# Tile 30's image-prompt softmax: which of its steps run on GpSimd and which on VectorE

## The chip, the core and the metric

The kernel runs on one core of a Trainium2 chip. The core has a matrix engine (TensorE, PE in the profile; PEld is its weight loads), three elementwise engines (VectorE = DVE, ScalarE = ACT, GpSimd = POOL) and SyncE (SP), which here only issues DMAs. Each engine runs its own instruction list in order; engines wait for each other through counting semaphores. An instruction whose semaphore has not arrived holds up everything behind it on its engine. The metric is the device time of one execution in microseconds, the median of several.

## The reference

Eight batches of 512 tokens with 320 channels attend, with 20 heads of 16 channels, to 60 text tokens and 4 image-prompt ("ip") tokens of 512 channels. Cut to what matters:

```python
q = heads(x @ W_q)
probs_t  = softmax(q @ k_t.T * scale)                 # 60 text tokens
text_out = probs_t @ v_t
qsem  = l2norm(probs_t @ text_ehs)                    # direction of the attended text
sem   = qsem @ l2norm(ip_ehs).T                       # 4 numbers a head
fused = q @ k_ip.T * scale + 0.5 * sem
probs_ip = softmax(fused) * spatial_mask              # over the 4 ip tokens
out = (text_out + probs_ip @ v_ip) @ W_out + b_out + x
```

The kernel takes the ip logits relative to the fourth ip token, so three numbers a head (60 columns for 20 heads) are computed and the fourth is a zero that was written once. The norm of `qsem` comes from a quadratic form of the unnormalised text probabilities with a 60x60 Gram matrix, one number a head.

## The kernel before, in words

The 4,096 tokens are 32 tiles of 128 (tiles 0 to 31). A tile is worked in five units of four heads, 160 units in all (units 0 to 159; tile 30 has units 150 to 154, tile 31 units 155 to 159). For each unit TensorE forms scores (`scores`), VectorE takes their maximum (`maxima`), ScalarE their exponentials (`exps`), TensorE transposes those (`e_transposes`), ScalarE copies them (`copy_eT`), TensorE multiplies them by a table of Gram matrix, ip directions and values (`table_products`), VectorE forms four quadratic forms (`quadratic`, line 795, one custom instruction and one accumulator read each), and ScalarE copies the rest of the product (`copy_fin`, line 628).

When a tile's five units are through, its end steps follow. Their names and lines:

- `clamp` on VectorE (lines 939, 942, 943): a guarded quadratic form, and the reciprocal of the text softmax's sum. From the first, ScalarE's `norms` (725, 727) makes the inverse norm, a logarithm and an exponential.
- `normalize` on GpSimd (516): the text part of the output row, written into `mixed` (320 columns).
- semn, sum, maximum, centring: ip directions times the inverse norm, plus the ip logits, their maximum over four, and the difference from it. On VectorE these are the four instructions of `centre` (949, 952, 954, 956); on GpSimd they are `fuse` (524, 527) and `centre` (533), with the maximum alone on VectorE (923).
- `weights` on ScalarE (732): the exponential.
- `weigh`: sum, reciprocal, weighting with the mask, written into `mixed` beside the text part. On VectorE three instructions (963, 965, 967); on GpSimd the last is two (541, 545), while sum and reciprocal stay on VectorE.
- Then TensorE transposes the row (`attn_transposes`, 1086), ScalarE copies it rounded (`attn_high`, 633), VectorE takes what rounding lost (`attnT_lows`, 877), TensorE multiplies by the output weights (`out_project`, 1108, nine matmuls), VectorE adds the residual (`add_residual`, 884) and SP stores the tile.

Tiles 0 to 27 go through the end steps in pairs, tiles 28 to 31 singly. Their groups are numbered in `POST`; `PLAIN` is 16, tile 30's group, and `PLAIN + 1` tile 31's. Before the change the GpSimd form of the end steps is used up to tile 29 (whose weighting is already on VectorE), and the VectorE form for tiles 30 and 31.

No scheduler sets the order. Each engine's list is written out in Python, as `slot(u)` calls with extra steps hung in at given values of `u`. Three orders matter at the end. On VectorE: `quadratic(156)`, `clamp` of tile 30, `quadratic(157)`, `centre` of tile 30, the residual of tile 28, `quadratic(158)`, `attnT_lows(29)`, `weigh` of tile 30, `quadratic(159)`, then the end steps of tile 31 with `attnT_lows(30)` ahead of their `centre`. On TensorE: `table_products(159)`, `attn_transposes(30)`, `out_project(29)`, `out_project(30)`, then the transposes and products of tile 31 (1115, 1123, 1125, 1128, 1130). `attn_transposes(30)` waits for `attn_made` and for `pip_made`, the semaphore that tile 30's weighting raises, and `out_project(29)` stands behind it. On GpSimd only the two `normalize` of tiles 30 and 31 remain.

Of the kernel before, what the change touches and what calls it, by code (L numbers as in the profile page):

```python
# [31 lines left out]
ALU = mybir.AluOpType  # L32
ACT = mybir.ActivationFunctionType
AX_X = mybir.AxisListType.X
# [10 lines left out]
def xattn_kernel(nc, x, ctx_tokens, ip_mask, w_q, w_k, w_v, w_k_ip, w_v_ip, w_out, b_out, out):  # L45
# [18 lines left out]
    ALL_UNITS, ALL_TILES, ALL_HALVES = B * UNITS, B * TILES, B * HALVES  # L64
# [11 lines left out]
    PLAIN = len(POST) - 2  # L76
# [4 lines left out]
    with es:  # L81
# [6 lines left out]
        def sem(name):  # L88
            return es.enter_context(nc.semaphore(name))
# [9 lines left out]
        def again(place, *shape):  # L99

            start = place_used.get(place.name, 0)
            place_used[place.name] = start + math.prod(shape)
            names = "abc"[:len(shape)]
            return place[:, start:start + math.prod(shape)].rearrange(
                f"p ({' '.join(names)}) -> p {' '.join(names)}", **dict(zip(names, shape)))
# [61 lines left out]
        fused = again(place_wq, TILES, HEADS, NIP)  # L167
        ipmax = again(place_ctxT, TILES, HEADS)
        ipd = again(place_wq, TILES, HEADS, NIP)
        ipe = again(place_ctxT, TILES, HEADS, NIP)  # L170
        ipsum = again(place_ctxT, TILES, HEADS)
        iprec = again(place_ctxT, TILES, HEADS)
# [53 lines left out]
        rnorm_made, semn_made, fused_made = sem("rnorm_made"), sem("semn_made"), sem("fused_made")  # L226
        attn_made, ipmax_made, ipd_made, ipe_made = (
            sem("attn_made"), sem("ipmax_made"), sem("ipd_made"), sem("ipe_made"))
        ipsum_made, iprec_made, ipw_made, pip_made = (
            sem("ipsum_made"), sem("iprec_made"), sem("ipw_made"), sem("pip_made"))  # L230
# [3 lines left out]
        end_step = sem("end_step")  # L234
# [33 lines left out]
        def ring(g):  # L268

            t, n = POST[g]  # L270
            return slice(t % TILES, t % TILES + n)
# [110 lines left out]
        def _(pool):  # L382
            g = nc.gpsimd
# [128 lines left out]
            def normalize(g):  # L512

                n, tiles = POST[g][1], ring(g)
                pool.wait_ge(rsum_made, g + 1)
                nc.gpsimd.tensor_tensor(  # L516
                    mixed[:, tiles, 0:C].rearrange("p t (h d) -> p t h d", d=D), fin[:, tiles, :, NDIF:NDIF + D],
                    rsum[:, tiles].unsqueeze(3).to_broadcast([P, n, HEADS, D]), ALU.mult).then_inc(attn_made, 1)
# [10 lines left out]
            def centre(g):  # L529

                n, tiles = POST[g][1], ring(g)
                pool.wait_ge(ipmax_made, g + 1)
                nc.gpsimd.tensor_tensor(ipd[:, tiles], fused[:, tiles], ipmax[:, tiles].unsqueeze(3).to_broadcast([P, n, HEADS, NIP]),
                                        ALU.subtract).then_inc(ipd_made, 1)

            def weigh(g):

                (t, n), tiles = POST[g], ring(g)
                pool.wait_ge(iprec_made, g + 1)
                pool.sem_inc(pool_turn, 1)  # L540
                nc.gpsimd.tensor_tensor(ipw[:, tiles], iprec[:, tiles],
                                        mask_sb[:, t % TILES:t % TILES + n].unsqueeze(2).to_broadcast([P, n, HEADS]),
                                        ALU.mult).then_inc(ipw_made, 1)
                pool.wait_ge(ipw_made, g + 1)
                nc.gpsimd.tensor_tensor(
                    mixed[:, tiles, C:C + IPCOLS].rearrange("p t (h n) -> p t h n", n=NDIF), ipe[:, tiles, :, 0:NDIF],
                    ipw[:, tiles].unsqueeze(3).to_broadcast([P, n, HEADS, NDIF]), ALU.mult).then_inc(pip_made, 1)
# [21 lines left out]
            for g in range(SINGLE // 2, PLAIN):  # L569
# [3 lines left out]
                fuse(g)  # L573
                centre(g)
            normalize(PLAIN)
            normalize(PLAIN + 1)


        @block.scalar
        def _(act):  # L580
# [49 lines left out]
            def attn_high(t):  # L630

                act.wait_ge(attnT_done, t + 1)
                nc.scalar.copy(attn_parts(t)[0], mi_ps[:, misc_bank(("at", 0, t)), 0:QC * P]).then_inc(attnT_hi, 1)
# [88 lines left out]
            def norms(g):  # L722

                act.wait_ge(quadc_made, g + 1)
                nc.scalar.activation(lnq[:, ring(g)], quadc[:, ring(g)], ACT.Ln).then_inc(lnq_made, 1)
                act.wait_ge(lnq_made, g + 1)
                nc.scalar.activation(rnorm[:, ring(g)], lnq[:, ring(g)], ACT.Exp, scale=-0.5).then_inc(rnorm_made, 1)

            def weights(g):

                act.wait_ge(ipd_made, g + 1)
                nc.scalar.activation(ipe[:, ring(g)], ipd[:, ring(g)], ACT.Exp).then_inc(ipe_made, 1)

            for u in range(ALL_UNITS + 2):
                slot(u)
                if u == ALL_UNITS - 2:
                    norms(PLAIN)
                if u == ALL_UNITS - 1:
                    weights(PLAIN)
            attn_high(ALL_TILES - 2)  # L740
            norms(PLAIN + 1)
            weights(PLAIN + 1)

            act.wait_ge(last_done, 1)
# [6 lines left out]
        def _(dve):  # L751
            v = nc.vector
# [120 lines left out]
            def attnT_lows(t):  # L873

                dve.wait_ge(attnT_hi, t + 1)
                high, low = attn_parts(t)
                v.tensor_tensor(low, mi_ps[:, misc_bank(("at", 0, t)), 0:QC * P], high.bitcast(F32), ALU.subtract).then_inc(attnT_lo, 1)
# [56 lines left out]
            def clamp(g):  # L934

                t = POST[g][0]
                dve.wait_ge(fin_copied, GROUPS * (t + 1))
                ssum = fin[:, ring(g), :, FINW - 1]
                v.scalar_tensor_tensor(out=guard[:, ring(g)], in0=ssum, scalar=EPS * EPS, in1=ssum,
                                       op0=ALU.mult, op1=ALU.mult).then_inc(guard_made, 1)  # L940
                dve.wait_ge(guard_made, g + 1)
                v.tensor_tensor(quadc[:, ring(g)], quad[:, ring(g)], guard[:, ring(g)], ALU.max).then_inc(quadc_made, 1)
                v.reciprocal(rsum[:, ring(g)], ssum).then_inc(rsum_made, 1)  # L943

            def centre(g):

                tiles, steps = ring(g), 3 * (g - PLAIN)
                dve.wait_ge(rnorm_made, g + 1)
                v.tensor_tensor(semn[:, tiles], fin[:, tiles, :, 0:NDIF],
                                rnorm[:, tiles].unsqueeze(3).to_broadcast([P, 1, HEADS, NDIF]), ALU.mult).then_inc(end_step, 1)  # L950
                dve.wait_ge(end_step, steps + 1)
                v.tensor_tensor(fused[:, tiles, :, 0:NDIF], semn[:, tiles], sip[:, tiles], ALU.add).then_inc(end_step, 1)
                dve.wait_ge(end_step, steps + 2)
                v.tensor_reduce(ipmax[:, tiles], fused[:, tiles], AX_X, ALU.max).then_inc(end_step, 1)
                dve.wait_ge(end_step, steps + 3)
                v.tensor_tensor(ipd[:, tiles], fused[:, tiles], ipmax[:, tiles].unsqueeze(3).to_broadcast([P, 1, HEADS, NIP]),
                                ALU.subtract).then_inc(ipd_made, 1)

            def weigh(g):

                t = POST[g][0]
                dve.wait_ge(ipe_made, g + 1)
                v.tensor_reduce(ipsum[:, ring(g)], ipe[:, ring(g)], AX_X, ALU.add).then_inc(ipsum_made, 1)
                dve.wait_ge(ipsum_made, g + 1)
                v.reciprocal(iprec[:, ring(g)], ipsum[:, ring(g)]).then_inc(iprec_made, 1)
                dve.wait_ge(iprec_made, g + 1)
                v.scalar_tensor_tensor(
                    out=mixed[:, t % ARING, C:C + IPCOLS].rearrange("p (h n) -> p h n", n=NDIF), in0=ipe[:, t % TILES, :, 0:NDIF],
                    scalar=mask_sb[:, t % TILES:t % TILES + 1], in1=iprec[:, t % TILES].unsqueeze(2).to_broadcast([P, HEADS, NDIF]),
                    op0=ALU.mult, op1=ALU.mult).then_inc(pip_made, 1)  # L970

            for u in range(ALL_UNITS + 1):
                slot(u)
                if u == ALL_UNITS - 4:
                    weigh(PLAIN - 1)
                if u == ALL_UNITS - 3:
                    clamp(PLAIN)
                if u == ALL_UNITS - 2:
                    centre(PLAIN)
                if u == ALL_UNITS - 1:  # L980
                    weigh(PLAIN)

            clamp(PLAIN + 1)
            attnT_lows(ALL_TILES - 2)
            centre(PLAIN + 1)
            weigh(PLAIN + 1)
            dve.wait_ge(last_hi, 1)
            v.tensor_tensor(last_attnT_low[:, 0:2 * P], LAST_ATTN[:, 0:2 * P], last_attnT[:, 0:2 * P].bitcast(F32),
# [302 lines left out]
```

## Time and profile before

| what | value |
|---|---|
| median of 3 runs | 318.04 us (317.91, 318.04, 320.0) |
| the profiled execution | 319.01 us, of which its span is 317.3 us |
| PE, DVE, ACT busy, share of the span | 95%, 85%, 87% |
| POOL busy | 66% |
| the change begins to act | about 305 us into the span |

The span runs from the first to the last instruction of the profiled execution; the 1.71 us beside it lie around it. Busy shares are averages over the whole span. The change touches only the last 13 us, where the shares are others: there the rows of single instructions, in order of time, say who waits for whom. Times in such rows are us from the span's start.

### The profile page before, as it was taken

How to read it: one execution, taken by the hardware profiler on the slowest of the kernel's cores; microseconds unless marked ns; L12 is line 12 of the kernel's file. 1: busy time of each engine (PE TensorE's matmuls, PEld its weight loads, DVE VectorE, ACT ScalarE, POOL GpSimd, SP SyncE). 2: the span in 40 equal slices, each digit the busy share in tenths (PEclk: the TensorE clock that was granted, in tenths of full speed). 3: DMA queues.
4: the chain of work that ended last, by engine and by line, in shares of the span. 5: the costliest groups of instructions: out<-in, count | busy, mean ns of one | idle time of the engine just before them, and what ended most of it. 6: DMA issues, size and time to landing. Idle time of an engine off the chain costs nothing.

```text
span 317.3 us, 8813 instructions
## 1 busy us (share of the span) xinstructions
PE 301.7 (95%) x2289; PEld 291.1 (92%) x2289; DVE 269.5 (85%) x1861; ACT 276.9 (87%) x1168; POOL 210.1 (66%) x372
## 2 busy tenths in 40 slices
PE   4899899999999999999999999999999999998976
PEld 3789769888999999999999999999999999998964
DVE  5483846798889898989898989998999899898995
ACT  3744679999999999999999999999999999999942
POOL 3033416687877789688977796889787878675200
PEclk9999999999999999999999999999999999999999
DMA  6980003000120202011110112021202120010011
GB/s 193 347 253 1 0 8 91 2 1 3 32 64 21 66 30 66 25 44 45 30 63 9 56 32 65 22 64 34 64 24 63 34 62 24 23 33 22 24 42 64
DMA packets 15130, 17.02 MB, mean 54 GB/s; under 512 B 2592, under 2 KB 14536, under 8 KB 15080
## 3 DMA queue, kind: packets, MB, share of 16 engines
q1 hardware_dynamic: 15080, 16.44, 17.1%
q8 instruction: 20, 0.33, 0.4%
q14 instruction: 30, 0.25, 0.2%
HBM read 10.55 MB, written 5.24 MB: 50 GB/s over the span
## 4 chain that ended last, share of the span: by engine, by line
PE 79%; DVE 8%; ACT 7%; DMA 2%; POOL 1%; issue 1%; SPq 1%; POOLq 0%
PE gv_ps L1073 23%; PE mi_ps L1108 12%; PE mi_ps L1032 12%; PE sc_ps L1052 10%; PE et_ps L1060 10%; ACT e_sb L619 4%; PE mi_ps L1086 3%; DMA x_nat<-in_x 2%; PE mi_ps L1010 2%; DVE place_ctxT L795 2%; PE gv_ps L1187 2%; PE mi_ps L1012 1%; DVE ktok L847 1%; PE sc_ps L1167 1%; DVE negmax L787 1%
## 5 line engine op out<-in xcount | busy, mean ns | idle before, releaser
L619 ACT ACTIVATE e_sb<-sc_ps,negmax 128x60 f32<-128x60 f32 x640 | 152.6, 353 | 6.3 <-DVE negmax L787 5.1
L795 DVE CUSTOM_DVE_ANT_0 place_ctxT<-gv_ps,e_sb 128x60 f32<-128x60 f32 x640 | 100.8, 213 | 16.9 <-PE gv_ps L1073 15.4
L1073 PE MATMUL gv_ps<-tab,place_w 128*128 128x160 f32 x640 | 113.1, 299 | 0.0
L1073 PEld LDWEIGHTS gv_ps<-tab,place_w 128*128 128x128 f32 x640 | 93.7, 189 | 0.3 <-ACT place_w L637 0.3
L1052 PE MATMUL sc_ps<-km,qs 128*128 128x256 f32 x320 | 77.0, 322 | 0.1
L637 ACT COPY place_w<-et_ps 128x256 f32<-128x256 f32 x160 | 68.5, 428 | 0.2
L1060 PE MATMUL et_ps<-ident,e_sb 128*128 128x128 f32 x320 | 61.9, 275 | 2.9 <-ACT e_sb L619 1.8
L787 DVE TENSOR_REDUCE negmax<-sc_ps 128x4 f32<-128x240 f32 x160 | 63.4, 397 | 0.0
L795 DVE DVE_READ_ACCUMULATOR2_ANT quad<- 128x1 f32 x640 | 52.5, 82 | 0.0
L420 POOL TENSOR_TENSOR km<-ktok,group_mask 128x512 fp32r<-128x512 f32 x40 | 41.3, 1039 | 14.4 <-DVE ktok L847 7.9
L628 ACT COPY fin<-gv_ps 128x80 f32<-128x80 f32 x160 | 43.8, 274 | 6.7 <-DVE quad L795 5.7
L1052 PEld LDWEIGHTS sc_ps<-km,qs 128*128 128x128 f32 x320 | 48.3, 191 | 0.5 <-issue 0.3
L1060 PEld LDWEIGHTS et_ps<-ident,e_sb 128*128 128x128 f32 x320 | 41.9, 141 | 6.7 <-ACT e_sb L619 5.4
L496 POOL TENSOR_TENSOR qs<-q_full,qs 64x256 fp32r<-64x256 f32 x60 | 43.7, 729 | 4.8
L494 POOL CAST qs<-q_full 64x256 fp32r<-64x256 f32 x60 | 23.5, 392 | 25.3 <-ACT q_full L597 23.3
L516 POOL TENSOR_TENSOR mixed<-fin,place_ctxT 128x640 f32<-128x640 f32 (+1 forms) x18 | 21.6, 1201 | 15.7 <-DVE place_ctxT L943 9.7
L786 DVE COPY sip<-sc_ps 128x12 f32<-128x12 f32 x160 | 26.1, 163 | 3.7 <-PE sc_ps L1052 3.1
L1108 PE MATMUL mi_ps<-wo_parts,attnT 128*128 128x320 f32 x120 | 22.8, 312 | 0.0
L884 DVE TENSOR_TENSOR place_w<-mi_ps,x_nat 128x320 f32<-128x320 f32 x31 | 14.9, 484 | 5.3 <-PE mi_ps L1108 5.3
L1108 PE MATMUL mi_ps<-wo_parts,attnT_low 128*128 128x320 f32 x60 | 19.1, 323 | 0.0
L433 POOL COPY tab<-g_sb 60x315 f32<-60x315 f32 x32 | 14.7, 459 | 6.5 <-POOL tab L433 3.1
L1032 PE MATMUL mi_ps<-xl,wq_hi 128*128 128x256 f32 (+1 forms) x96 | 19.0, 279 | 0.0
(184 smaller groups left out, 557.2 us busy)
## 6 DMA issues: line engine op xcount, KB each, us to landing
x_nat<-in_x SPq DMA_DIRECT2D x16, 320.0 KB, 3.2
out<-place_w SPq DMA_DIRECT2D x32, 160.0 KB, 1.8
place_ctx<-in_ctx SPq DMA_DIRECT2D x4, 256.0 KB, 3.3
place_w<-in_L_xattn_W_v SPq DMA_DIRECT2D x1, 640.0 KB, 8.0
place_w<-in_L_xattn_W_k SPq DMA_DIRECT2D x1, 640.0 KB, 9.4
place_w<-in_L_xattn_W_k_ip SPq DMA_DIRECT2D x1, 640.0 KB, 11.0
place_w<-in_L_xattn_W_v_ip SPq DMA_DIRECT2D x1, 640.0 KB, 9.5
place_ctxT<-in_L_xattn_W_out SPq DMA_DIRECT2D x1, 640.0 KB
```

The lines of the kernel that those rows point to most:

```text
L420: g.tensor_tensor(km[:, b % 2, c].rearrange("p s (j t) -> p s j t", t=TOK), ktok[:, :, c, TOK * b:TOK * b + TOK].unsqueeze(2).to_broadcast ...
L496: g.tensor_tensor(qs[other, half % 2, c, :], q_full[own, m, :], qs[own, half % 2, c, :].bitcast(F32), ALU.subtract).then_inc(q_part, 1)
L619: last = nc.scalar.activation(e_sb[:, slot, TOK * j:TOK * j + T], sc_ps[:, bank, TOK * j:TOK * j + T], ACT.Exp, bias=negmax[:, slot, j:j + 1])
L628: nc.scalar.copy(fin[:, t % TILES, GROUP * c:GROUP * c + GROUP, :], ps[:, :, T:TABW]).then_inc(fin_copied, 1)
L637: nc.scalar.copy(eT[:, u % TRING, :], et_ps[:, u % 2, 0:2 * P]).then_inc(eT_copied, 1)
L787: v.tensor_reduce(negmax[:, u % ERING, :], ps[:, :, 0:T], AX_X, ALU.max, negate=True).then_inc(max_done, 1)
L795: last = v.tensor_tensor_reduce(out=junk[:, u % 2, j, 0:T], in0=gv_ps[:, u % 2, TABW * j:TABW * j + T], in1=e_sb[:, u % ERING, TOK * j:TOK ...
L1032: last = mm(to, w, xx, start=n == 0, stop=n == len(steps) - 1)
L1052: last = mm(sc_ps[:, u % 2, 0:GROUP * TOK], q, km[:, parity, c, part, :], start=part == 0, stop=part == 1)
L1060: last = tr(et_ps[:, u % 2, P * r:P * r + P], e_sb[:, u % ERING, P * r:P * r + P], ident[:])
L1073: last = mm(gv_ps[:, u % 2, 2 * TABW * r:2 * TABW * r + 2 * TABW], eT[:, u % TRING, P * r:P * r + P], tab[:, b % 2, h:h + 2, :].rearrange( ...
L1108: last = mm(ps, steps[n][0], steps[n][1], start=n == 0, stop=n == len(steps) - 1)
```

## The change

For tile 30, semn, sum, centring and the two steps of the weighting are issued on GpSimd (`fuse`, `centre` and `weigh`, between the two last `normalize`). VectorE keeps the maximum, placed behind `slot(159)`'s work and so between `quadratic(158)` and `quadratic(159)`, and sum and reciprocal, placed behind `quadratic(159)` and ahead of tile 31's `clamp`. ScalarE's exponential of tile 30 moves one slot later, and its `norms` of tile 31 go ahead of `attn_high(30)`. On VectorE `attnT_lows(30)` goes behind tile 31's `centre`.

```diff
@@ weigh, on gpsimd @@
-                pool.wait_ge(ipw_made, g + 1)
+                pool.wait_ge(ipw_made, min(g + 1, PLAIN))
@@ end of the gpsimd list @@
             normalize(PLAIN)
+            fuse(PLAIN)
+            centre(PLAIN)
+            weigh(PLAIN)
             normalize(PLAIN + 1)
@@ end of the scalar list @@
                 if u == ALL_UNITS - 2:
                     norms(PLAIN)
-                if u == ALL_UNITS - 1:
+                if u == ALL_UNITS:
                     weights(PLAIN)
+            norms(PLAIN + 1)
             attn_high(ALL_TILES - 2)
-            norms(PLAIN + 1)
             weights(PLAIN + 1)
@@ centre, on vector: steps counted from 1, now for tile 31 alone @@
-                tiles, steps = ring(g), 3 * (g - PLAIN)
+                tiles = ring(g)
...
@@ end of the vector list @@
                 if u == ALL_UNITS - 3:
                     clamp(PLAIN)
-                if u == ALL_UNITS - 2:
-                    centre(PLAIN)
                 if u == ALL_UNITS - 1:
-                    weigh(PLAIN)
-
+                    dve.wait_ge(fused_made, PLAIN + 1)
+                    v.tensor_reduce(ipmax[:, ring(PLAIN)], fused[:, ring(PLAIN)], AX_X, ALU.max).then_inc(ipmax_made, 1)
+
+            dve.wait_ge(ipe_made, PLAIN + 1)
+            v.tensor_reduce(ipsum[:, ring(PLAIN)], ipe[:, ring(PLAIN)], AX_X, ALU.add).then_inc(ipsum_made, 1)
+            dve.wait_ge(ipsum_made, PLAIN + 1)
+            v.reciprocal(iprec[:, ring(PLAIN)], ipsum[:, ring(PLAIN)]).then_inc(iprec_made, 1)
             clamp(PLAIN + 1)
+            centre(PLAIN + 1)
             attnT_lows(ALL_TILES - 2)
-            centre(PLAIN + 1)
             weigh(PLAIN + 1)
```

The GpSimd list at its end, now (`place_wq` holds semn, the sum and the centred values, `place_ctxT` the maximum, reciprocals and exponentials):

```order
L516 TENSOR_TENSOR mixed<-fin,place_ctxT 128x320 [waits rsum_made]
L524 TENSOR_TENSOR place_wq<-fin,place_ctxT 128x60 [waits rnorm_made]
L527 TENSOR_TENSOR place_wq<-place_wq,sip 128x20x3 [waits semn_made]
L533 TENSOR_TENSOR place_wq<-place_wq,place_ctxT 128x80 [waits ipmax_made]
L541 TENSOR_TENSOR ipw<-place_ctxT,mask_sb 128x20 [waits iprec_made]
L545 TENSOR_TENSOR mixed<-place_ctxT,ipw 128x60 [waits ipw_made]
L516 TENSOR_TENSOR mixed<-fin,place_ctxT 128x320 [waits rsum_made]
```

Before, the two rows of line 516 followed each other; five instructions now stand between them, and tile 31's `normalize` is behind all five.

The VectorE list from `attnT_lows(29)` on, before (the four pairs of line 795 of `quadratic(159)` follow the third of these rows):

```order
L877 TENSOR_TENSOR attnT_low<-mi_ps,attnT 128x384 [waits attnT_hi]
L963 TENSOR_REDUCE place_ctxT<-place_ctxT 128x20 [waits ipe_made]
L965 RECIPROCAL place_ctxT<-place_ctxT 128x20 [waits ipsum_made]
L967 SCALAR_TENSOR_TENSOR mixed<-place_ctxT,mask_sb 128x60 [waits iprec_made]
L795 ISA place_ctxT,quad<-gv_ps,e_sb 128x60 [waits gv_done]
```

and now, the same stretch, where line numbers are 3 to 6 higher (`quadratic` is line 798):

```order
L880 TENSOR_TENSOR attnT_low<-mi_ps,attnT 128x384 [waits attnT_hi]
L983 TENSOR_REDUCE place_ctxT<-place_wq 128x20 [waits fused_made]
L798 ISA place_ctxT,quad<-gv_ps,e_sb 128x60 [waits gv_done]
```

with, behind `quadratic(159)`, sum and reciprocal of tile 30 and then tile 31's steps:

```order
L986 TENSOR_REDUCE place_ctxT<-place_ctxT 128x20 [waits ipe_made]
L988 RECIPROCAL place_ctxT<-place_ctxT 128x20 [waits ipsum_made]
L942 SCALAR_TENSOR_TENSOR place_ctxT<-fin 128x20 [waits fin_copied]
L945 TENSOR_TENSOR place_ctxT<-quad,place_ctxT 128x20 [waits guard_made]
L946 RECIPROCAL place_ctxT<-fin 128x20
L952 TENSOR_TENSOR place_wq<-fin,place_ctxT 128x60 [waits rnorm_made]
L955 TENSOR_TENSOR place_wq<-place_wq,sip 128x20x3 [waits end_step]
L957 TENSOR_REDUCE place_ctxT<-place_wq 128x20 [waits end_step]
L959 TENSOR_TENSOR place_wq<-place_wq,place_ctxT 128x80 [waits end_step]
L880 TENSOR_TENSOR u_all<-mi_ps,xh 128x384 [waits attnT_hi]
```

Tile 30's weighting was finished ahead of `quadratic(159)`; now its reciprocal is formed behind it and the weighting itself on GpSimd. The last row is `attnT_lows(30)`, which stood ahead of tile 31's four `centre` steps. TensorE's list is the same in both.

## Rows read from the trace of the kernel before

**Rows 1.** TensorE in order of time: start us, us, instruction, [idle before, releaser].

```profile
305.45 0.49 PE L1086 MATMUL mi_ps<-ident,mixed 128*128 128x128 f32 x3
...
308.66 0.52 PE L1086 MATMUL mi_ps<-ident,mixed 128*128 128x128 f32 x3 [2.17 <-DVE mixed L967]
...
310.19 0.31 PE L1108 MATMUL mi_ps<-u_all,attnT_low 128*128 128x320 f32 x1
310.56 0.82 PE L1108 MATMUL mi_ps<-wo_parts,xh 128*128 128x320 f32 x4
...
311.38 0.38 PE L1115 MATMUL sc_ps<-ident,mixed 128*128 128x128 f32 x2
...
312.33 0.86 PE L1123 MATMUL et_ps<-wo_parts,xh 128*128 128x320 f32 x4
313.03 0.28 PE L1125 MATMUL sc_ps<-ident,mixed 128*128 128x128 f32 x1
...
313.71 0.76 PE L1130 MATMUL et_ps<-place_ctxT,place_w 128*128 128x320 f32 x2
```

**Rows 2.** VectorE in order of time, the stretch of tiles 30 and 31.

```profile
305.07 0.49 DVE L949 TENSOR_TENSOR place_wq<-fin,place_ctxT 128x60 f32<-128x60 f32 x1
...
307.23 0.55 DVE L877 TENSOR_TENSOR attnT_low<-mi_ps,attnT 128x384 fp32r<-128x384 f32 x1
307.70 0.23 DVE L963 TENSOR_REDUCE place_ctxT<-place_ctxT 128x20 f32<-128x80 f32 x1
307.96 0.28 DVE L965 RECIPROCAL place_ctxT<-place_ctxT 128x20 f32<-128x20 f32 x1
308.27 0.28 DVE L967 SCALAR_TENSOR_TENSOR mixed<-place_ctxT,mask_sb 128x60 f32<-128x60 f32 x1
...
309.41 0.20 DVE L939 SCALAR_TENSOR_TENSOR place_ctxT<-fin 128x20 f32<-128x20 f32 x1 [0.29 <-ACT fin L628]
...
309.74 0.27 DVE L943 RECIPROCAL place_ctxT<-fin 128x20 f32<-128x20 f32 x1
309.93 0.49 DVE L877 TENSOR_TENSOR u_all<-mi_ps,xh 128x384 fp32r<-128x384 f32 x1
310.36 0.56 DVE L949 TENSOR_TENSOR place_wq<-fin,place_ctxT 128x60 f32<-128x60 f32 x1
...
311.48 0.24 DVE L956 TENSOR_TENSOR place_wq<-place_wq,place_ctxT 128x80 f32<-128x80 f32 x1
312.06 0.24 DVE L963 TENSOR_REDUCE place_ctxT<-place_ctxT 128x20 f32<-128x80 f32 x1 [0.34 <-ACT place_ctxT L732]
```

**Rows 3.** ScalarE in order of time, the same stretch.

```profile
305.98 0.48 ACT L633 CAST attnT<-mi_ps 128x384 fp32r<-128x384 f32 x1 [0.57 <-PE mi_ps L1086]
...
310.10 0.22 ACT L727 ACTIVATE place_ctxT<-place_ctxT 128x20 f32<-128x20 f32 x1
311.75 0.27 ACT L732 ACTIVATE place_ctxT<-place_wq 128x80 f32<-128x80 f32 x1 [1.43 <-DVE place_wq L956]
311.93 0.35 ACT L745 CAST xh<-sc_ps 128x256 fp32r<-128x256 f32 x1
```

**Rows 4.** GpSimd in order of time: steps of tiles 28, 29, 30 and 31.

```profile
295.58 0.22 POOL L541 TENSOR_TENSOR ipw<-place_ctxT,mask_sb 128x20 f32<-128x20 f32 x1
295.88 0.29 POOL L545 TENSOR_TENSOR mixed<-place_ctxT,ipw 128x60 f32<-128x60 f32 x1
...
299.29 0.33 POOL L533 TENSOR_TENSOR place_wq<-place_wq,place_ctxT 128x80 f32<-128x80 f32 x1 [0.98 <-DVE place_ctxT L923]
...
304.73 0.76 POOL L516 TENSOR_TENSOR mixed<-fin,place_ctxT 128x320 f32<-128x320 f32 x1 [5.11 <-DVE place_ctxT L943]
310.09 0.75 POOL L516 TENSOR_TENSOR mixed<-fin,place_ctxT 128x320 f32<-128x320 f32 x1 [4.61 <-DVE place_ctxT L943]
```

**Rows 5.** Stretches: us, busy of PE, PEld, DVE, ACT, POOL, then PEclk (granted clock).

```profile
306.00:308.60 2.60, 0.49 (x4) 0.24 (x2) 2.50 (x16) 0.89 (x3) 0.00 (x0) 1.00 0.19 66
308.60:311.00 2.40, 2.28 (x15) 2.08 (x16) 2.04 (x14) 1.04 (x4) 0.75 (x1) 1.00 0.00 0
```

More of the change, by code:

```diff
@@ L950, in centre @@
                                 rnorm[:, tiles].unsqueeze(3).to_broadcast([P, 1, HEADS, NDIF]), ALU.mult).then_inc(end_step, 1)
-                dve.wait_ge(end_step, steps + 1)
+                dve.wait_ge(end_step, 1)
                 v.tensor_tensor(fused[:, tiles, :, 0:NDIF], semn[:, tiles], sip[:, tiles], ALU.add).then_inc(end_step, 1)
-                dve.wait_ge(end_step, steps + 2)
+                dve.wait_ge(end_step, 2)
                 v.tensor_reduce(ipmax[:, tiles], fused[:, tiles], AX_X, ALU.max).then_inc(end_step, 1)
-                dve.wait_ge(end_step, steps + 3)
+                dve.wait_ge(end_step, 3)
                 v.tensor_tensor(ipd[:, tiles], fused[:, tiles], ipmax[:, tiles].unsqueeze(3).to_broadcast([P, 1, HEADS, NIP]),
```

## The prediction, made before the result was known

> **What bounds the kernel now.** The change acts in the last 13 us only, so I went from the page's busy shares straight to TensorE's own row of instructions at the end [rows 1], then to the engines that it waits for there [rows 2 to 4]. TensorE's shares (95% of the span) say nothing about this stretch: in 306 to 308.6 us it works 0.49 us of 2.60 while VectorE works 2.50 [rows 5]. The reader is to see one long wait in it: `attn_transposes(30)` starts at 308.66 after 2.17 idle, released by VectorE's line 967, the weighting of tile 30 [rows 1]. That wait is `pip_made`. From 308.66 to the end of line 1130 at 313.71 + 0.76 = 314.47 TensorE then runs with hardly a gap: `out_project(29)` is queued behind the transposes, `out_project(30)` behind that. So **the time at which tile 30's weighting is done sets the start of a 5.8 us stream of matmuls that ends the kernel**. VectorE is the second chain of about the same length: it is busy from tile 30's end steps up to tile 31's, and the stream meets it at 310.56 (`out_project(30)` waits for `attnT_lows(30)`, which ended at 309.93 + 0.49 = 310.42) and at 312.33 (the copy at 311.93 + 0.35 = 312.28) [rows 1 to 3].
>
> **The change, part by part.** Times are on the profiled execution's scale.
>
> *Prices of a hand-over*, from the end of one instruction to the start of the next that waited for it: VectorE to GpSimd 0.08 (309.74 + 0.27 to 310.09), GpSimd to itself 0.08 (295.58 + 0.22 to 295.88), VectorE to ScalarE 0.03 (311.48 + 0.24 to 311.75), ScalarE to VectorE 0.04 (311.75 + 0.27 to 312.06), VectorE to TensorE 0.11 (308.27 + 0.28 to 308.66), TensorE to ScalarE 0.04 (305.45 + 0.49 to 305.98) [rows 1 to 4]. GpSimd to ScalarE and to TensorE have no row of their own; they lie between 0.03 and 0.11, and I take 0.04 and 0.11, what the same receivers need from others. An instruction of VectorE that waits for nothing starts 0.08 before its forerunner's end (309.93 against 310.01) [rows 2].
>
> *Taken from VectorE:* for tile 30 semn 0.49, the sum, centring 0.24 and weighting 0.28 [rows 2], some 1.2 us. Of this, what lies ahead of `quadratic(158)` saves nothing: `quadratic(158)` and the residual need TensorE's products, and `attnT_lows(29)` needs ScalarE's copy, which ends at 305.98 + 0.48 = 306.46 as before [rows 3].
>
> *semn and sum on GpSimd:* no cost. They start behind `normalize` of tile 30, which ends at 304.73 + 0.76 = 305.49 [rows 4]; two instructions below 0.33 each and two hand-overs end them near 306.2, while their reader on VectorE stands behind `attnT_lows(29)` until 306.97. Cover of 0.8 us.
>
> *The new chain of tile 30,* step by step. `attnT_lows(29)` 306.46 + 0.04 = 306.50 to 307.05 (0.55; before it ran at 307.23). Maximum from 306.97, priced as the equal reduction 0.23: 307.20. GpSimd centring +0.08, 0.33 (line 533 on tile 29): 307.61. ScalarE's exponential +0.04, 0.27: 307.92. Sum on VectorE +0.04, start to start 0.26 to the reciprocal (307.70 to 307.96), 0.28: 308.50. `quadratic(159)` runs in the gap between 307.12 and the sum, so it costs nothing. GpSimd's mask step +0.08, 0.22, then +0.08, 0.29: 309.17. TensorE +0.11: **`attn_transposes(30)` starts at 309.28 instead of 308.66, 0.62 later** [rows 2 to 4]. Before, the same weighting took three neighbours on VectorE; now the chain changes engines five times, and its six hand-overs add up to some 0.4 us.
>
> Here the rows and a rule differ. GpSimd needs 0.33 for the centring against VectorE's 0.24, and 0.22 + 0.29 for the weighting against 0.28 [rows 2, 4]: 1.4 and 1.8 times. The Trainium skill (GPSIMD Engine Reference, sections 3 and 4) says that two-input elementwise work is about twice as slow on GpSimd and belongs on VectorE; doubled VectorE rows would be 0.48 and 0.56, an estimate, and would put the start 0.2 later than rows do. The trace has durations for both lines, so I use them.
>
> *Tile 31 on VectorE,* earlier: its `clamp` starts 308.42 instead of 309.41. From that start the rsum needed by `normalize` ended after 0.60 (310.01), and the inverse norm after 0.91 (310.10 + 0.22) [rows 2, 3]: 309.02 and 309.33. But `normalize` of tile 31 now stands behind the weighting on GpSimd: 309.17 to 309.92. And line 949 is not free while GpSimd reads: at 305.07 and 310.36 it took 0.49 and 0.56 and ended at 305.56 and 310.92, both times 0.07 to 0.08 after GpSimd's line 516 (305.49, 310.84) [rows 2, 4]. So I let it end at 309.92 + 0.08 = 310.00. The other three ended 0.80 later (311.48 + 0.24 = 311.72 against 310.92): 310.80.
>
> *`attnT_lows(30)`, moved behind them:* its input is ready at 309.28 + 0.52 + 0.04 + 0.48 = 310.32, it starts at 310.72 and ends at 311.21. `out_project(30)` +0.14, as before: 311.35, 0.79 later. TensorE alone would be ready at 310.19 + 0.17 + 0.62 = 310.98 (0.17 a matmul: four from 312.33 to 313.03), so the new order costs at most 0.37 here, at least nothing.
>
> *The rest of the stream.* Line 1115 moves by 0.79 and ends at 311.38 + 0.38 + 0.79 = 312.55. Before, ScalarE was still on tile 31's exponential until 311.75 + 0.27 = 312.02 and copied late; that exponential now ends near 311.1, so the copy runs 312.59 to 312.94 and line 1123 starts 0.05 behind, as before, at 312.99, 0.66 later. Line 1125, which waited for tile 31's weighting, waits for nothing now (0.03 less): 0.63 later, and line 1130, the last residual and the last store follow. **Sum: +0.6 us.** Tile 31's VectorE chain ends some 0.9 us earlier than before and buys 0.15 of this back.
>
> Bounds: +0.25 if `attnT_lows(30)` comes in time (0.37 less); +1.0 with GpSimd's two missing hand-overs and a blocked instruction (below). The profiled execution, 319.01, becomes 319.6; it lies 0.97 above the median shown, the difference is around and in the span alike, so I add to the median: 318.04 + 0.6 = **318.6 us**. The three runs lie between 317.91 and 320.0, and a median can move by several tenths for that alone.
>
> **The rivals.**
>
> *1. VectorE's freed time wins; not slower.* Place: `attn_transposes(30)`. If its start stayed at 308.66, `out_project(30)` would no longer wait (310.36 instead of 310.56) and line 1123 would start near 312.0: some 0.4 us faster, 317.6. It decides at 308.6 for the end of the weighting. Against it: even with every hand-over ahead of TensorE's at zero the weighting ends at 308.85. For it: VectorE is busy 2.50 of 2.60 us there [rows 5], and each 0.1 us counts both ways.
>
> *2. GpSimd is blocked by VectorE.* The lock seen on line 949 could work the other way: `clamp` of tile 31 starts at 308.42 with two instructions of two inputs each from the on-chip memory, done 0.41 later (309.74 + 0.08 against 309.41) [rows 2], and GpSimd's mask step wants to start at 308.58. If it waits for the second's end, the weighting, the transposes and the stream come 0.25 later: +0.85, 318.9. The Trainium skill (SBUF — State Buffer, "Who interferes with whom") says that a VectorE instruction with two inputs from this memory and a GpSimd instruction that reads it contend for a shared pair of ports, and that this is an exclusive lock; by that VectorE, which starts first, would hold GpSimd off here, and the two ends of line 949 agree for the other direction.
>
> *3. Slower for good: TensorE's clock falls.* TensorE's idle time ahead of 308.66 grows from 2.17 to 2.8 us. The granted clock was 1.00, the 2.4 GHz level, after the 2.17 [rows 1, 5]; should it fall to 1.2 GHz for half to all of the 5.8 us stream, the end comes 2.9 to 5.8 us later: 321.5 to 324.4. It decides once the idle stretch is long enough for a fall, and no row shows one at 2.17.
>
> That the change doesn't do what it says is excluded by the order of instructions; whether tile 30's work is off VectorE's list is not in doubt.
>
> **How the numbers follow.** Forecast (+0.25 to +0.8) 0.62; rival 1, no later or earlier, 0.17; rival 2 (+0.8 to +1.1) 0.15; rival 3 0.04; 0.02 for what I don't see, on both sides. A measurement of this kernel can tell about 1%, 3.2 us, from no change. Only rival 3 leaves that band: slower 0.05, faster 0.01, same 0.94. Range: 317.6 (rival 1) to 319.8 (rival 2's 319.1 and the scatter of a median of runs that reach 320.0).
>
> **What would show it.** Right: the three matmuls of `attn_transposes(30)` near 309.3 after 2.8 idle, released by GpSimd's second weighting step; that step near 308.9; line 949's counterpart for tile 31 still ending 0.08 after `normalize`; `out_project(30)` released by `attnT_lows(30)` near 311.3; the last residual 0.6 later. Wrong: a start at 308.7 or before (rival 1), a mask step of over 0.4 us or a late one (rival 2), PEclk below 1.00 behind 309 (rival 3), or any difference ahead of 305 us, where I see no cause for one.

## The result and the profile after

The changed kernel takes 320.2 us, the kernel before 318.64, each the median of 22 runs: a ratio of 1.0039 with a 95% interval of 1.0020 to 1.0057, slower by about 1.2 us (the two medians differ by 1.56 us, the means, 320.00 and 318.59, by 1.41; the ratios here and below are not those of the medians). The forecast was 318.6 (+0.6), its range ended at 319.8, so the result lies outside it. The sign was right; the size was at least twice the forecast, and the rival that I gave 0.04, a fall of TensorE's clock, is part of it.

Each run also has a mean granted TensorE clock over its span. By that number the runs of the changed kernel fall into groups, and those of the kernel before as well (its 70 runs are those taken beside the experiments, on two chips):

| kernel | clock 1.000 | clock 0.995 | clock 0.989 |
|---|---|---|---|
| changed, 22 runs | 6, median 318.82 | 13, median 320.31 | 3, median 321.46 |
| before, 70 runs | 34, medians 317.84 and 317.97 | 31, medians 319.19 and 319.07 | 5, medians 321.06 and 320.91 |

So the clock falls in 16 of 22 runs of the changed kernel, and in 36 of 70 of the kernel before, whose one traced execution was at 1.000. A step of 0.005 in the mean clock costs 1.1 to 1.5 us, two steps 2.6 to 3.2. No execution at 0.989 was traced, so where its second step lies is not known.

TensorE at the end of the changed kernel, in order of time, as in [rows 1] (line numbers are 6 higher; the last of these lines are the last products):

```profile
305.60 0.71 PE L1079 MATMUL gv_ps<-tab,place_w 128*128 128x160 f32 x4
309.17 0.52 PE L1092 MATMUL mi_ps<-ident,mixed 128*128 128x128 f32 x3 [2.86 <-issue]
309.44 1.03 PE L1114 MATMUL mi_ps<-wo_parts,attnT 128*128 128x320 f32 x4
...
311.61 1.27 PE L1114 MATMUL mi_ps<-wo_parts,xh 128*128 128x320 f32 x4
...
313.97 0.86 PE L1129 MATMUL et_ps<-wo_parts,xh 128*128 128x320 f32 x4
...
315.30 0.81 PE L1136 MATMUL et_ps<-place_ctxT,place_w 128*128 128x320 f32 x2
```

Tile 30's transposes start after 2.86 us of idling instead of 2.17, and four matmuls of `out_project(30)` take 1.27 us where they took 0.82 at the same line before. The profile names no releaser for that wait ("issue"); the transposes start 0.11 behind the end of GpSimd's second weighting step (line 545 below, 309.06), the same hand-over as behind VectorE's weighting before. The stretches of the same profile (us, busy time of PE, PEld, DVE, ACT, POOL, then the granted clock, DMA share, GB/s) say why:

```profile
306.00:308.60 2.60, 0.31 (x3) 0.06 (x1) 2.16 (x17) 0.81 (x5) 0.45 (x2) 1.00 0.18 63
308.60:311.00 2.40, 1.83 (x10) 1.86 (x11) 1.95 (x6) 1.16 (x4) 1.10 (x3) 0.77 0.00 0
311.00:313.00 2.00, 2.00 (x10) 1.96 (x9) 0.83 (x4) 0.00 (x0) 0.00 (x0) 0.50 0.03 8
313.00:315.00 2.00, 2.00 (x14) 1.83 (x12) 1.05 (x3) 0.40 (x2) 0.00 (x0) 0.92 0.00 0
```

The granted clock is 1.00 while TensorE idles, 0.50 (1.2 GHz) in the middle of the stream that follows, and 1.00 again near the end. In the traced execution of the kernel before it was 1.00 in the same stretches, [rows 5] and these two:

```profile
311.00:313.00 2.00, 2.00 (x14) 1.69 (x13) 1.52 (x7) 0.53 (x2) 0.00 (x0) 1.00 0.03 8
313.00:315.00 2.00, 1.47 (x7) 0.71 (x5) 1.54 (x4) 0.27 (x1) 0.00 (x0) 1.00 0.22 79
```

The Trainium skill (TensorE: Matmul & The Clock Gate, Part 1) describes such a gate, closed by idling and opened by work; the rows agree as to its two levels.

GpSimd and VectorE in the changed kernel:

```profile
307.09 0.33 POOL L533 TENSOR_TENSOR place_wq<-place_wq,place_ctxT 128x80 f32<-128x80 f32 x1 [1.16 <-DVE place_ctxT L983]
308.48 0.22 POOL L541 TENSOR_TENSOR ipw<-place_ctxT,mask_sb 128x20 f32<-128x20 f32 x1 [1.06 <-DVE place_ctxT L988]
308.77 0.29 POOL L545 TENSOR_TENSOR mixed<-place_ctxT,ipw 128x60 f32<-128x60 f32 x1
309.03 0.76 POOL L516 TENSOR_TENSOR mixed<-fin,place_ctxT 128x320 f32<-128x320 f32 x1
```

```profile
306.31 0.56 DVE L880 TENSOR_TENSOR attnT_low<-mi_ps,attnT 128x384 fp32r<-128x384 f32 x1 [0.19 <-ACT attnT L636]
306.78 0.23 DVE L983 TENSOR_REDUCE place_ctxT<-place_wq 128x20 f32<-128x80 f32 x1
...
308.02 0.28 DVE L988 RECIPROCAL place_ctxT<-place_ctxT 128x20 f32<-128x20 f32 x1
...
309.08 0.78 DVE L952 TENSOR_TENSOR place_wq<-fin,place_ctxT 128x60 f32<-128x60 f32 x1 [0.35 <-ACT place_ctxT L730]
...
310.58 0.55 DVE L880 TENSOR_TENSOR u_all<-mi_ps,xh 128x384 fp32r<-128x384 f32 x1
```

Every duration of the new chain is the one priced, to 0.01 us, and tile 31's semn (line 952) again ends 0.07 behind GpSimd's line 516 (309.86 against 309.79). One hand-over was priced wrong: from the reciprocal (line 988) to GpSimd's mask step (line 541) it took 0.18 us, not 0.08. The trace of the kernel before has 0.18 for the same step of an earlier tile too (286.69 to 286.87); its cause is not shown.

### The profile page after: what moved, and what is told of

Read it like the earlier page. It is cut to its first block, busy times and chain, and to the rows that moved or that the text cites. A ratio compares the mean times of both kernels' runs of the same rounds, so it can differ in the third digit from the quotient of the medians.

```text
span 318.9 us, 8815 instructions
## 1 busy us (share of the span) xinstructions
PE 303.1 (95%) x2289; PEld 292.3 (92%) x2289; DVE 269.0 (84%) x1857; ACT 277.6 (87%) x1168; POOL 212.2 (67%) x377
## 4 chain that ended last, share of the span: by engine, by line
PE 79%; ACT 8%; DVE 6%; issue 2%; DMA 2%; POOL 1%; SPq 1%; POOLq 0%
PE gv_ps L1079 23%; PE mi_ps L1114 12%; PE mi_ps L1038 12%; PE sc_ps L1058 10%; PE et_ps L1066 9%; ACT e_sb L622 5%; PE mi_ps L1092 3%; PE mi_ps L1016 2%; PE gv_ps L1193 2%; DMA place_ctx<-in_ctx 2%; DVE place_ctxT L798 1%; PE mi_ps L1018 1%; DVE negmax L790 1%; ACT place_w L640 1%; DVE ktok L850 1%
## 5 line engine op out<-in xcount | busy, mean ns | idle before, releaser
L640 ACT COPY place_w<-et_ps 128x256 f32<-128x256 f32 x160 | 69.2, 432 | 0.2
```

The costliest lines, as they stand in the source:

```text
L640: nc.scalar.copy(eT[:, u % TRING, :], et_ps[:, u % 2, 0:2 * P]).then_inc(eT_copied, 1)
```

## The experiments

The executions start their last part up to 2.5 us apart from one another, for reasons at their beginning (in the kernel before, TensorE starts the products of line 1151 at 11.63; in e3_order, below, it starts the same products at 9.11). So the traces are compared over the **tail**: from the start of the matmuls of `table_products(159)` (305.78 before) to the end of the last matmul (314.47), 8.69 us. Of the kernel before this is the first row, which [rows 1] leaves out:

```profile
305.78 0.71 PE L1073 MATMUL gv_ps<-tab,place_w 128*128 128x160 f32 x4
```

| kernel | tile 30's transposes, from the tail's start | idle stretches ahead of tile 30's or `out_project(30)`'s matmuls, us | tail of the traced execution, its clock | runs below 0.998 |
|---|---|---|---|---|
| before | 2.88 | 2.17 | 8.69, 1.000 | 36 of 70 |
| changed | 3.57 | 2.86 | 10.51, 0.995 | 16 of 22 |
| e1_warm | 3.58 | 1.12, 0.26 | 9.47, 1.000 | 0 of 12 |
| e2_late | 3.52 | 2.82 | 10.45, 0.995 | 11 of 12 |
| e3_order | 3.57 | 2.86 | 9.13, 1.000 | 8 of 12 |
| e4_swap | 3.57 | 0.71, 0.59, 1.58 | 10.88, 0.993 | 9 of 12 |
| e5_before_warm | 2.87 | 0.42 | 8.68, 0.999 | 0 of 12 |
| e6_fill | 3.58 | 0.16, 0.60, 0.46 | 8.59, 0.999 | 1 of 12 |
| e7_weigh | 3.12 | 0.66, 0.89 | 9.64, 1.000 | 0 of 12 |
| e8_order_warm | 3.58 | 1.12 | 9.13, 0.999 | 0 of 12 |

**e1_warm: the idle stretch filled.** On the changed kernel:

```diff
                 if kind == "at":
+                    if index == ALL_TILES - 2:
+                        for _ in range(16):
+                            tr(BANKS[3][:, 0:P], ident[:], ident[:])
                     attn_transposes(index)
```

> The changed kernel, with 16 extra transposes of the identity into a free bank on TensorE, ahead of tile 30's transposes: they fill the idle stretch (2.86 us) and change nothing else. Theory 1 (the longer idle stretch lets TensorE's clock fall in most executions, and the fall is most of the loss): granted clock 1.000 in every run, tile 30's transposes at the same distance from tile 29's, time 0 to 0.6 us above the kernel before (ratio 1.000 to 1.002). Theory 2 (the loss is the longer chain of hand-overs and the new order on VectorE, the clock is a bystander): still 1.0 to 1.6 us above it (ratio 1.003 to 1.005).

Median 318.74 beside 318.83 for the kernel before, ratio 1.0014 (0.9994 to 1.0035), the clock between 0.998 and 1.000 in all 12 runs, as theory 1 expected. TensorE's rows:

```profile
304.79 0.71 PE L1079 MATMUL gv_ps<-tab,place_w 128*128 128x160 f32 x4
305.34 1.91 PE L1263 MATMUL et_ps<-ident 128*128 128x128 f32 x16
308.37 0.52 PE L1092 MATMUL mi_ps<-ident,mixed 128*128 128x128 f32 x3 [1.12 <-issue]
...
310.47 0.82 PE L1114 MATMUL mi_ps<-wo_parts,xh 128*128 128x320 f32 x4 [0.26 <-DVE u_all L880]
...
313.45 0.81 PE L1136 MATMUL et_ps<-place_ctxT,place_w 128*128 128x320 f32 x2
```

The transposes come as late as in the changed kernel (3.58), but the four matmuls of `out_project(30)` take 0.82 again. The tail is 9.47 instead of 10.51: 1.04 us of the traced execution's loss was the clock. What is left at full clock is 9.47 - 8.69 = 0.78 us. In the medians it reads larger: the runs of the kernel before at 1.000, taken beside these, have 317.84, 0.9 below.

**e2_late: the idle stretch lengthened without GpSimd.** On the kernel before (the line that makes the scratch buffer is left out here):

```diff
                 if u == ALL_UNITS - 1:
+                    v.tensor_reduce(scratch[:], wo[:, 0:2, 0:280], AX_X, ALU.max)
                     weigh(PLAIN)
```

> The kernel before, with one extra reduction of 560 columns on VectorE ahead of tile 30's weighting (about 0.7 us), and no GpSimd in it: TensorE's idle stretch grows from 2.2 to about 2.85 us. Theory 1: the clock falls in more than half of the runs (about 0.995), time 1.3 to 2.3 us above the kernel before (ratio 1.004 to 1.007). Theory 2: clock 1.000, time 0.4 to 0.9 us above it (1.001 to 1.003).

Median 319.77, ratio 1.0040 (1.0015 to 1.0066): as slow as the changed kernel, with none of tile 30's steps moved to GpSimd. The clock fell in 11 of 12 runs. The trace:

```profile
305.06 0.71 PE L1076 MATMUL gv_ps<-tab,place_w 128*128 128x160 f32 x4
308.58 0.52 PE L1089 MATMUL mi_ps<-ident,mixed 128*128 128x128 f32 x3 [2.82 <-DVE mixed L969]
308.86 1.32 PE L1111 MATMUL mi_ps<-wo_parts,attnT 128*128 128x320 f32 x4
...
314.70 0.81 PE L1133 MATMUL et_ps<-place_ctxT,place_w 128*128 128x320 f32 x2
```

The reduction of 0.73 us put the transposes off by 0.64; the tail grew by 1.76; the other 1.12 is the clock. Theory 1 was right on the share of falls; the time is at the lower end of its range by the ratio and below it by the medians (0.94 us). The runs of the kernel before taken beside these show falls too (16 of 35), which neither theory had in it.

**e3_order: the order on VectorE undone**, on the changed kernel:

```diff
             clamp(PLAIN + 1)
-            centre(PLAIN + 1)
             attnT_lows(ALL_TILES - 2)
+            centre(PLAIN + 1)
```

> The changed kernel with attnT_lows(30) put back ahead of tile 31's centre on VectorE. Theory 1: the idle stretch is as long as in the changed kernel, the clock still falls in most runs, time 0.6 to 1.6 us above the kernel before. Theory 2, by which the order on VectorE is a good part of the loss: at least 0.4 us below the changed kernel, 0.3 to 0.9 us above the kernel before, whatever the clock does.

Median 319.58, ratio 1.0015 (0.9988 to 1.0042), the clock low in 8 of 12 runs. By the medians (0.75 us above) both theories allow the time, by the ratio (0.5) only theory 2; the trace, which fell on an execution at 1.000, decides more: a tail of 9.13 behind an idle stretch of 2.86. The fall is thus not certain after 2.86, and the order costs 0.34 beside e1_warm.

**e4_swap: `out_project(29)` moved into the idle stretch.** In `slot`, `out_project(29)` is called ahead of `attn_transposes(30)` and left out of its own slots (the two conditions that do this are not shown):

```diff
+                if kind == "at" and index == ALL_TILES - 2:
+                    out_project(ALL_TILES - 3, 0)
+                    out_project(ALL_TILES - 3, 1)
                 if kind == "at":
                     attn_transposes(index)
```

> The changed kernel, with out_project(29) issued ahead of tile 30's transposes on TensorE, same banks: the nine matmuls fill most of the idle stretch (0.5 to 0.9 us stay), and the stream behind the transposes is shorter by 1.6 us. Theory 1: clock 1.000, and since out_project(30) then starts as soon as attnT_lows(30) is done, 0.2 to 0.9 us faster than the kernel before (ratio 0.997 to 0.9995). Theory 2: tile 30's transposes come as late as in the changed kernel and out_project(30) waits for attnT_lows(30) as there, so at most 0.4 us better than the changed kernel: 0.7 to 1.2 us above the kernel before.

Median 319.9, ratio 1.0033 (1.0008 to 1.0059): theory 1 was wrong here in both numbers, and theory 2 right in the time. The matmuls did fill most of the first stretch, but another opened behind the transposes:

```profile
304.77 0.71 PE L1079 MATMUL gv_ps<-tab,place_w 128*128 128x160 f32 x4
306.18 0.83 PE L1114 MATMUL mi_ps<-wo_parts,attnT 128*128 128x320 f32 x4 [0.71 <-DVE attnT_low L880]
...
308.34 0.52 PE L1092 MATMUL mi_ps<-ident,mixed 128*128 128x128 f32 x3 [0.59 <-issue]
310.45 1.26 PE L1114 MATMUL mi_ps<-wo_parts,xh 128*128 128x320 f32 x4 [1.58 <-DVE u_all L880]
```

`out_project(30)` now waits 1.58 for `attnT_lows(30)`, and starts 5.68 behind the tail's start, as in e1_warm. The clock fell in 9 of 12 runs although no single stretch was longer than 1.58. It fell only behind the start of `out_project(30)` in the trace (1.00 from 310.00 to 310.45). **In the changed kernel's order, then, `attnT_lows(30)` sets the start of `out_project(30)` at full clock, whether `out_project(29)` stands ahead of the transposes or behind them.**

**e5_before_warm: the kernel before, filled** with the edit of e1_warm.

> The kernel before, with the same 16 extra transposes of the identity ahead of tile 30's transposes. In the first four runs the kernel before itself had the lower granted clock in 16 of 35 executions (median 319.2 and above, against 317.8 at 1.000). Theory 1 (any idle stretch of 2.2 us or more there lets the clock fall in a share of the executions that grows with its length): granted clock 0.998 or more in every run, median 317.5 to 318.1, ratio 0.996 to 0.9985. Theory 2 (the split of the kernel before has another cause, at its start or between executions): the same split, ratio 0.999 to 1.001.

Median 317.65 beside 318.78, ratio 0.9977 (0.9957 to 0.9997), the clock at 0.999 or 1.000 in all 12 runs and the tail unchanged at 8.68; theory 1 was right in all of it. The traced execution, at 0.999, has its fall behind the last matmul (at 313.60), where it costs nothing:

```profile
304.92 0.71 PE L1073 MATMUL gv_ps<-tab,place_w 128*128 128x160 f32 x4
...
312.84 0.76 PE L1130 MATMUL et_ps<-place_ctxT,place_w 128*128 128x320 f32 x2
```

```profile
313.00:315.00 2.00, 0.60 (x3) 0.09 (x1) 0.67 (x2) 0.00 (x0) 0.00 (x0) 1.00 0.48 167
315.00:316.30 1.30, 0.00 (x0) 0.00 (x0) 0.00 (x0) 0.00 (x0) 0.00 (x0) 0.70 0.34 121
```

So the falls of the kernel before belong to its 2.17 us of idling in the same place, and the extra transposes take them away. This version is 0.2% faster than the kernel before, by an interval that only just excludes no change.

**e6_fill: useful work instead of extra transposes.** The changed kernel with e4_swap's order, five extra transposes, and `out_project(30)` behind the first four products of tile 31; on ScalarE the copy of tile 31's transposes goes ahead of tile 31's exponential. Shown is the last step on TensorE alone:

```diff
                 for k in range(4):
                     mm(LAST_OUT, steps[k][0], steps[k][1], start=k == 0, stop=False)
+                out_project(ALL_TILES - 2, 0)
+                out_project(ALL_TILES - 2, 1)
```

> The changed kernel with TensorE's last work reordered: five extra transposes and out_project(29) ahead of tile 30's transposes, then tile 31's transposes and first four products, and only then out_project(30); ScalarE's copy of tile 31's transposes ahead of its exponential. No idle stretch over 0.7 us stays. Theory 1: clock 0.998 or more in every run, 7.9 to 8.4 us from the start of table_products(159) to the last matmul's end (before 8.69, extra transposes in the changed kernel 9.47), median 317.0 to 317.7, ratio 0.9945 to 0.9975. Theory 2 (the chain of hand-overs to attnT_lows(30) and tile 31's weighting ends last whatever TensorE does): 9.0 or more, no faster than the kernel before.

Median 318.12, ratio 0.9991 (0.9965 to 1.0017): a tail of 8.59, between what the theories expected. Tile 31's transposes come right behind tile 30's, but ScalarE's copies and `attnT_lows(30)` end only near 310, and TensorE has nothing else by then:

```profile
308.19 0.52 PE L1091 MATMUL mi_ps<-ident,mixed 128*128 128x128 f32 x3 [0.60 <-issue]
308.85 0.44 PE L1120 MATMUL sc_ps<-ident,mixed 128*128 128x128 f32 x2
309.75 0.86 PE L1128 MATMUL et_ps<-wo_parts,xh 128*128 128x320 f32 x4 [0.46 <-ACT xh L746]
310.44 0.75 PE L1113 MATMUL mi_ps<-wo_parts,xh 128*128 128x320 f32 x4
```

It wins back the whole loss of the change at full clock, and one run of 12 still had a clock of 0.989, two steps down; it was not traced.

**e7_weigh: the weighting back on VectorE**, on e1_warm. GpSimd's `weigh(PLAIN)` is left out, and behind `quadratic(159)`:

```diff
-            dve.wait_ge(ipe_made, PLAIN + 1)
-            v.tensor_reduce(ipsum[:, ring(PLAIN)], ...
-            dve.wait_ge(ipsum_made, PLAIN + 1)
-            v.reciprocal(iprec[:, ring(PLAIN)], ...
+            weigh(PLAIN)
             clamp(PLAIN + 1)
```

> The changed kernel with the 16 extra transposes, and tile 30's weighting back on VectorE (semn, sum and centring stay on GpSimd). If GpSimd's two weighting instructions and their hand-overs are what makes tile 30's transposes late: 3.2 to 3.3 us from the start of table_products(159) to them (3.58 with the weighting on GpSimd, 2.88 before), 9.0 to 9.2 us to the last matmul's end instead of 9.47, 0.2 to 0.5 us faster than the changed kernel with extra transposes. If the loss at full clock is line 949's counterpart blocked by GpSimd on tile 31: the transposes 0.3 earlier all the same, but 9.4 or more to the end.

Median 319.11, ratio 1.0015 (0.9989 to 1.0041). The transposes start 0.46 earlier (3.12), and the tail gets longer all the same: 9.64 against 9.47. TensorE's and VectorE's rows:

```profile
304.89 0.71 PE L1075 MATMUL gv_ps<-tab,place_w 128*128 128x160 f32 x4
...
308.01 0.52 PE L1088 MATMUL mi_ps<-ident,mixed 128*128 128x128 f32 x3 [0.66 <-issue]
...
313.72 0.81 PE L1132 MATMUL et_ps<-place_ctxT,place_w 128*128 128x320 f32 x2
```

```profile
307.82 0.19 DVE L941 SCALAR_TENSOR_TENSOR place_ctxT<-fin 128x20 f32<-128x20 f32 x1
...
308.76 0.57 DVE L951 TENSOR_TENSOR place_wq<-fin,place_ctxT 128x60 f32<-128x60 f32 x1 [0.35 <-ACT place_ctxT L729]
...
310.05 0.55 DVE L879 TENSOR_TENSOR u_all<-mi_ps,xh 128x384 fp32r<-128x384 f32 x1
```

The weighting puts tile 31's `clamp` and with it `centre` off, and `attnT_lows(30)` is queued behind them: it starts 5.16 behind the tail's start instead of 4.98, though its input was there earlier. So the two weighting instructions on GpSimd do make the transposes late, as the first reading had it, but its tail of 9.0 to 9.2 was wrong. The second reading fits the tail, though the block by GpSimd is only a part of it: line 951 takes 0.57 here and 0.78 in e1_warm, but starts 0.38 later in the tail.

**e8_order_warm: e3's order on e1_warm.**

> The changed kernel with the 16 extra transposes and attnT_lows(30) ahead of tile 31's centre. If the order on VectorE costs what the one look at full clock showed: 9.05 to 9.25 us from table_products(159) to the last matmul's end (9.47 with the new order), median 0.2 to 0.5 below that kernel. If TensorE's stream was not waiting for attnT_lows(30): 9.4 or more, and no difference.

Median 318.51, ratio 0.9993 (0.9971 to 1.0016); the tail is 9.13, as the first reading expected and the same as in e3_order. With `attnT_lows(30)` first, VectorE waits for its input, and semn comes when GpSimd has been done since 308.97:

```profile
304.79 0.71 PE L1079 MATMUL gv_ps<-tab,place_w 128*128 128x160 f32 x4
...
313.11 0.81 PE L1136 MATMUL et_ps<-place_ctxT,place_w 128*128 128x320 f32 x2
```

```profile
308.22 0.75 POOL L516 TENSOR_TENSOR mixed<-fin,place_ctxT 128x320 f32<-128x320 f32 x1
```

```profile
309.43 0.56 DVE L880 TENSOR_TENSOR u_all<-mi_ps,xh 128x384 fp32r<-128x384 f32 x1 [1.50 <-ACT xh L636]
309.91 0.21 DVE L952 TENSOR_TENSOR place_wq<-fin,place_ctxT 128x60 f32<-128x60 f32 x1
```

Line 952 takes 0.21 alone and 0.78 beside GpSimd's line 516. The Trainium skill (SBUF — State Buffer, "Who interferes with whom") calls the pair of ports that the two share an exclusive lock; this pair of rows agrees with it.

## Why the prediction was wrong, point by point

- **The chain of tile 30: right.** Forecast 0.62 later, measured 0.69 (3.57 against 2.88); the rest is the hand-over to the mask step, 0.18 instead of 0.08. GpSimd's durations were the ones of the rows (0.33, 0.22, 0.29), not twice VectorE's.
- **The stream behind it at full clock: right in kind, 0.15 short.** Forecast +0.63, measured 0.78 by the tails of e1_warm and the kernel before: the rest is a later `out_project(30)` (5.68 against 4.78, +0.90; forecast +0.79), because `attnT_lows(30)` starts 0.04 later than forecast and takes 0.55 instead of 0.49. The order's cost, bounded by 0.37, is 0.34 (e8_order_warm). So at full clock +0.34 is the new order, and +0.44 the rest, with transposes that come 0.69 later.
- **"TensorE's clock falls", 0.04 and "no row shows one at 2.17": this step failed.** The sum had no term for the clock, because one traced execution at 1.00 was read as what every execution does. In fact the clock falls in half of the runs behind 2.17 us of idling already, and in 35 of 46 behind 2.82 to 2.86 us (16 of 22 here, 11 of 12 in e2_late, 8 of 12 in e3_order). The price was mis-sized too: I took half to all of a stream of 5.8 us, 2.9 to 5.8; a fall costs 1.04 to 1.41 in the traces (10.51 and, in e4_swap, 10.88, against 9.47), since the clock is back before the stream ends, and 1.1 to 1.5 in the medians.
- **The sum as it should have been.** At full clock +0.8 (tails) to +0.9 (medians, 318.82 against some 317.9). The falls add (13 x 1.49 + 3 x 2.64)/22 = 1.24 on average to the changed kernel and some (31 x 1.2 + 5 x 3.05)/70 = 0.75 to the kernel before, a difference of 0.5. Together 1.3 to 1.4 us; measured, 1.2 by the ratio (0.0039 of 318.64) and 1.4 by the means. In medians the falls weigh more, because a median jumps from one level to the next: 318.64 lies between the levels of the kernel before, 320.2 lies at the changed kernel's level of 0.995.
- **The baseline.** 318.04, the median of three runs, was 0.6 below the median of 22. By their times the three lay on both sides of the split, which I took for scatter, and the range left too little room for it on the slow side. The 1% that I said a measurement can tell from no change was too wide as well: a change of 0.4% was told.
- **Rival 1** did not happen: the transposes came later. VectorE's freed time is there (tile 31's weighting ends 6.30 us behind the tail's start, 7.14 before) and nothing waits for it any more. **Rival 2** did not either: GpSimd's mask step took its 0.22, and its start was 0.10 late by a hand-over that the kernel before shows as well.

Shown are the fall, its cure by filled idle time, its cause without GpSimd, and the order's cost. Not shown is which executions fall, nor where the second step of those at 0.989 lies. No fall of the kernel before was traced; there its runs' mean clocks and e5_before_warm stand for it.

## What to carry to other kernels

A wait of TensorE near the end costs no more than its length only while the clock holds. Here, behind waits of 2.2 to 2.9 us, the clock fell in half to three quarters of the runs, and filling the wait with matmuls that nobody needs took away most of the loss (ratio 1.0014 instead of 1.0039) without shortening the chain that causes it. Before a median is explained, look at the granted clock of every run: one trace shows one of several cases. And a step moved to an idle engine must be followed to everything queued behind its last instruction: here the additional hand-overs, and `attnT_lows(30)` behind `centre`, cost more than the freed engine saved.

## What the runs showed of the hardware that was not expected

- The clock fell in e4_swap in 9 of 12 runs with gaps of 0.71, 0.59 and 1.58 us and 2.1 us of matmuls between them; with gaps of at most 1.12 us (e1_warm, e5_before_warm, e7_weigh, e8_order_warm) no run of 48 was below 0.998. A short longest gap was not a guarantee: e6_fill, with none over 0.60 in its trace, had one run of 12 at 0.989.
- A VectorE instruction with both inputs in the on-chip memory took 0.21 us alone and 0.78 beside a GpSimd instruction that reads there, ending 0.07 behind it; the reductions of line 787 (0.40 us in the trace of the kernel before) and the quadratic forms (0.21 to 0.22 in the changed kernel) took as long beside GpSimd as alone.
